# The FFN's LayerNorm tiles (`hbuf`) written by GpSimd instead of ScalarE

## The chip, the cores and the metric

The kernel runs on one core of one Trainium2 chip. The core has five engines that work side by side and meet only at semaphores: TensorE (PE; PEld is its weight load), VectorE (DVE), ScalarE (ACT), GpSimd (POOL) and SyncE (SP), the last of which only issues transfers here. Each engine takes its instructions strictly in the order in which they are written. The metric is device time in microseconds (us), median of several runs.

## What is computed

A cross-attention layer and a feed-forward layer with a learned memory, on 16 tiles of 128 tokens x 1024. Cut to what matters here:

```python
x = x + xattn(layernorm(x), ctx, ...)          # first layer
h = layernorm(x)                               # (x - mean) / sqrt(var + eps), per row
q = h @ Wq.T                                   # 64 columns
learned = gelu(h @ Wu1.T + bu1) @ Wu2.T + bu2  # 256 hidden columns
# router scores from q, top 8 of 256 slots, softmax, value rows -> aux_out
x = x + (h + gate * aux_out)                   # second layer
```

So the second LayerNorm `h` is needed twice: as the operand of a product with 320 columns (256 for `Wu1`, 64 for `Wq`), and in the sum `x + h`.

## The kernel before, in words

`X[:, b, :]` holds tile `b` (b = 0 to 15) for the whole run. The attention part runs as a software pipeline over periods `b` of four steps `i`; in period `b` the keys of tile `b`, the queries of tile `p = b - 1`, the output of tile `o = b - 2` and the normalisation of tile `e = b - 3` are worked on. There are 19 periods, so that periods 16, 17 and 18 (`B`, `B+1`, `B+2`) drain the pipeline.

The first part of the FFN, the "hidden steps", begins in period `B+1`: `early_step(b, i)` gives step 0 for `(B+1, 0)` up to step 7 for `(B+2, 3)`; steps 8 to 16 follow alone. In hidden step `s`:

- TensorE transposes `hbuf` of tile `s+1` (`h_transpose`, L543, 8 transposes into the PSUM tile `k_slot` or `q_slot`), and then multiplies tile `s` (`hidden_products`, L556, 24 matmuls of 320 columns; three per block, since operands are split in a high and a low half).
- ScalarE copies the transposed tile `s+1` out of PSUM rounded (`hT_high`, L788), runs the gelu of tile `s-1` (L792), writes `hbuf` of tile `s+2` (`h_scale`, L782: `X*rstd2 + nb2`, where `nb2 = -mean*rstd2`), and sums the weighted gelu of tile `s-1` (`unit_sum`, L796).
- VectorE makes the low half (`hT_low`, L1155), multiplies the gelu by `Wu2` (`unit_weights`, L1172, both inputs in SBUF), and adds the bias to the product of tile `s` (`unit_bias`, L1161).
- GpSimd writes `x + h` into `X` in place (`hidden_sum`, L1001: `X*(1+rstd2) + nb2`), once `h_done` says that `hbuf` has been made from the old `X`.

`hbuf` has two buffers, taken in turn, so tile `b` may be written once the transposes of tile `b-2` are done (semaphore `h_T`).

Tiles 0 and 1 are made earlier: `h_scale(0)` at the end of period `B`, after which TensorE does `h_transpose(0)` right after its last `o_pair` (L504) of that period, and `h_scale(1)` at the start of period `B+1`. GpSimd's own work at that place is `q_scale` (L967, which the transposes `q_turn` L465 wait for), a `memset` of `q_rows` (L1052), `mt_bias` (L973, which the next `o_pair` waits for), `rstd2_pow` (L987 to L994: `rstd2`, `nb2` and `1+rstd2` of one tile, five small instructions) and `norm_scale` (L978 to L982, which `o_turn` L512 waits for).

In period `B+1`, step 2, TensorE's `o_pair` has to wait until ScalarE has emptied the PSUM tile `ob` (`o_copy`, L758), and ScalarE does that after its `unit_sum`.

After the hidden steps comes a tail of top-8 selection, softmax, and output products for the 16 tiles.

Of the kernel before, what the change touches and what calls it, by code (L numbers as in the profile page):

```python
# [6 lines left out]
ALU = mybir.AluOpType  # L7
ACT = mybir.ActivationFunctionType
# [3 lines left out]
B = 16  # L12
# [24 lines left out]
def wait(engine, sem, value):  # L37

    if value > 0:
        engine.wait_ge(sem, value)  # L40
# [7 lines left out]
def attention_ffn_kernel(nc, x, ctx_rows, ctx_cols, WqT_raw, WkT_raw, Wv_rows, WoT_rows, bo_row, g_col, Wuq_cols,  # L48
# [3 lines left out]
    with ctx:  # L52
# [7 lines left out]
        X = sb("x_all", [P, B, N])  # L60
# [4 lines left out]
        rstd2 = sb("rstd2", [P, B, 1])  # L65
        nb2 = sb("nb2", [P, B, 1])
# [68 lines left out]
        hbuf = sb("hbuf", [P, 2, N], scope=ffn)  # L135
# [55 lines left out]
        def early_step(b, i):  # L191
            return 4 * (b - B - 1) + i
# [72 lines left out]
        k_moved = [sem(f"k_moved{k}") for k in range(2)]  # L265
# [31 lines left out]
        rstd2_done = sem("rstd2_done")  # L297
# [13 lines left out]
        h_done = sem("h_done")  # L311
# [46 lines left out]
        def moved(b):  # L358

            return MOVED * b - MOVED // 2 if b else 0  # L360
# [353 lines left out]
        def _(act):  # L714
# [61 lines left out]
                    last = nc.scalar.mul(mt_sb[:, b % 2, t, :], gm[:, t * C:(t + 1) * C], kscale[:, t:t + 1])  # L776
                last.then_inc(mt_copied, 1)

            def h_scale(b, k):
                act.wait_ge(nb2_done, b + 1)  # L780
                wait(act, h_T, b - 1)
                nc.scalar.activation(hbuf[:, k, :], X[:, b, :], ACT.Identity, bias=nb2[:, b, :],  # L782
                                     scale=rstd2[:, b, :]).then_inc(h_done, 1)

            def hT_high(b, k):
                act.wait_ge(h_T, b + 1)
                wait(act, units_prod, b - 1)
# [11 lines left out]
            def hidden_step(b):  # L799
                if b + 1 < B:  # L800
                    hT_high(b + 1, (b + 1) % 2)
                if has(b - 1):
                    unit_gelu(b - 1, (b - 1) % 2)
                if b + 2 < B:
                    h_scale(b + 2, b % 2)
                if b == EARLY + 3:
                    act.wait_ge(varh_step, 2)
                    nc.scalar.activation(logv[:, :], varh[:, :], ACT.Ln, bias=ones[:, 0:1]).then_inc(logv_done, 1)
                if 0 < b < B:
                    unit_sum(b - 1, (b - 1) % 2)  # L810
# [14 lines left out]
            for b in range(PERIODS):  # L825
                p, o, e = b - 1, b - 2, b - 3
                for i in range(4):
                    if i == 0 and has(o):
                        mt_scale(o)
                    if i == 0 and has(e):  # L830
                        o_copy(e, 1)
                    if i == 2 and has(o):
                        o_copy(o, 0)
                    if b == B + 1 and i == 0:
                        act.wait_ge(q_prod, 4 * B)
                        act.wait_ge(m_prod, B)
                        hT_high(0, 0)
                        h_scale(1, 1)
                    qb, qi = (p, i - 1) if i else (o, 3)
                    if has(qb):  # L840
                        q_exponential(qb, qi)
                    if 0 < b < B:
                        k_exponential(b, i)
                    if i == 1 and 0 < b and has(b + 1):
                        ctx_high(b + 1)
                    qb, qi = (p, i - 2) if i >= 2 else (o, i + 2)
                    if has(qb):
                        if qb == 0 and qi == 0:
                            act.wait_ge(k_weights, 2)
                            act.wait_ge(q_weights, 2)  # L850
                        q_copy(qb, qi)
                    if i == 0 and has(e):
                        o_square(e, 1)
                    if i == 3 and has(o):
                        o_square(o, 0)
                    if i == 1 and 0 < b < B:
                        x_layernorm(b)
                    if i == 2:
                        if has(p):
                            g_copy(p)  # L860
                        if 0 < b < B:
                            x_high(b)
                    if b == 1 and i == 0:
                        act.wait_ge(u_prod, 1)
                        nc.scalar.copy(U[:, :, :].rearrange("p h c -> p (h c)"), turn[:, :]).then_inc(u_done, 1)
                    if b == 1 and i == 1:
                        act.wait_ge(vv_prod, NSLOT // P)
                        act.wait_ge(rk_prod, 1)
                        nc.scalar.copy(VV[:, :, :].rearrange("p s (r d) -> p s r d", d=VB),
                                       ob[:, 0:2 * VB].rearrange("p (s d) -> p s d", d=VB).unsqueeze(2).broadcast_to(  # L870
                                           [P, NSLOT // P, P // VB, VB])).then_inc(vv_copied, 1)
                        nc.scalar.copy(rkT, ob[0:RDIM, NSLOT:2 * NSLOT]).then_inc(rk_copied, 1)
                        act.wait_ge(score_zeros, 1)
                        nc.scalar.mul(scoreB[0:BOT, NSLOT:2 * NSLOT], keysT,
                                      float(BOT) ** -0.5).then_inc(score_ready, 1)
                    if b == 1 and i == 3:
                        act.wait_ge(b1_prod, 1)
                        nc.scalar.mul(scoreB[0:BOT, 0:NSLOT], ob[0:BOT, 0:NSLOT],
                                      float(RDIM) ** -0.5).then_inc(score_ready, 1)
                    if b == B and i == 0:  # L880
                        act.wait_ge(k_prod, 4 * B)
                        act.wait_ge(ctx_lo_done, B)
                        nc.scalar.dma_start(Wuq_in[:, :, :], Wuq_cols).then_inc(wuq_in, 16)
                    if b == B and i == 1:
                        act.wait_ge(k_prod, 4 * B)
                        act.wait_ge(wuq_in, 16)
                        nc.scalar.copy(WuqT[0][:, :, :], Wuq_in[:, :, :]).then_inc(wuq_hi, 1)
                    if b == B and i == 3:
                        for half in range(2):
                            act.wait_ge(k_moved[half], moved(B))  # L890
                        h_scale(0, 0)
                    if early_step(b, i) >= 0:
                        hidden_step(early_step(b, i))

# [46 lines left out]
        def _(pool):  # L941
# [43 lines left out]
            def rstd2_pow(b):  # L985
# [7 lines left out]
                nc.gpsimd.tensor_scalar(nb2[:, b, :], mr2[:, :], -1.0, None, ALU.mult).then_inc(nb2_done, 1)  # L993
                nc.gpsimd.tensor_scalar(one_rstd2[:, b, :], rstd2[:, b, :], 1.0, None, ALU.add).then_inc(one_rstd2_done, 1)  # L994

            def hidden_sum(b):

                pool.wait_ge(h_done, b + 1)
                pool.wait_ge(nb2_done, b + 1)
                pool.wait_ge(one_rstd2_done, b + 1)  # L1000
                nc.gpsimd.tensor_scalar(X[:, b, :], X[:, b, :], one_rstd2[:, b, :], nb2[:, b, :], ALU.mult,  # L1001
                                        ALU.add).then_inc(y_done, 1)
# [26 lines left out]
            for b in range(PERIODS):  # L1029
                p, o, e = b - 1, b - 2, b - 3  # L1030
                for i in range(4):
                    if i == 0 and has(o):
                        mt_bias(o)
                    if i == 3 and 0 < b < B:
                        x_low(b)
                    if early_step(b, i) == 0:
                        hidden_sum(0)
                    qb, qi = (p, i - 1) if i else (o, 3)
                    if has(qb):
                        q_scale(qb, qi)  # L1040
                    if i == 0 and 0 < b < B:
                        rstd_pow(b)
                    if i == 0 and has(e - 1):
                        rstd2_pow(e - 1)
                    if i == 1 and b > 0 and has(b + 1):
                        ctx_low(b + 1)
                    if i == 1 and has(e):
                        norm_scale(e)
                    if b == B and i == 3:
                        for half in range(2):  # L1050
                            pool.wait_ge(k_moved[half], moved(B))
                        nc.gpsimd.memset(q_rows[:, :, BOT:P], 1.0).then_inc(query_ones, 1)  # L1052
                    if early_step(b, i) > 0:
                        hidden_sum(early_step(b, i))
            rstd2_pow(B - 1)
# [6 lines left out]
                                        ALU.mult).then_inc(oscale_done, 1)  # L1062

            for b in range(EARLY, B):
                hidden_sum(b)
                if b == EARLY + 2:
                    pool.wait_ge(wvu_hi, 1)
                    nc.gpsimd.tensor_tensor(WvuT_lo[:, :], WvuT_in[:, :], WvuT_hi[:, :].bitcast(F32),
                                            ALU.subtract).then_inc(wvu_lo, 1)
# [363 lines left out]
```

## Time and profile before

| what | value |
|---|---|
| median of 3 runs | 640.03 us (640.01 to 640.49) |
| the profiled execution's own time | 640.05 us |
| its span in the trace | 638.1 us |
| PE busy | 615.7 us (96%) |
| DVE busy | 540.2 us (85%) |
| ACT busy | 416.9 us (65%) |
| POOL busy | 371.7 us (58%) |
| chain that ended last | PE 92% of the span |

The 1.95 us between the span and the execution's own time lie around the profile. The chain of waits is followed back from the last instruction; where it is nearly all one engine, that engine's order and pauses set the time, and the other engines' loads matter only where that engine waits for them. The hidden steps with the start of their preparation lie between 500 and 589 us of the span.

### The profile page before, as it was taken

How to read it: one execution, taken by the hardware profiler on the slowest of the kernel's cores; microseconds unless marked ns; L12 is line 12 of the kernel's file. 1: busy time of each engine (PE TensorE's matmuls, PEld its weight loads, DVE VectorE, ACT ScalarE, POOL GpSimd, SP SyncE). 2: the span in 40 equal slices, each digit the busy share in tenths (PEclk: the TensorE clock that was granted, in tenths of full speed). 3: DMA queues.
4: the chain of work that ended last, by engine and by line, in shares of the span. 5: the costliest groups of instructions: out<-in, count | busy, mean ns of one | idle time of the engine just before them, and what ended most of it. 6: DMA issues, size and time to landing. Idle time of an engine off the chain costs nothing.

```text
span 638.1 us, 11806 instructions
## 1 busy us (share of the span) xinstructions
PE 615.7 (96%) x3974; PEld 541.3 (85%) x3974; DVE 540.2 (85%) x757; ACT 416.9 (65%) x844; POOL 371.7 (58%) x369
## 2 busy tenths in 40 slices
PE   4899999999999999999999999999999999999796
PEld 3778888888888988888888988888888999999574
DVE  5989898989989898989898989898986745756997
ACT  5566676666666766666676767676664866773793
POOL 4954464848474748474747575756646456421394
PEclk9999999999999999999999999999999999999999
DMA  8943543444444444444444344543245100000056
GB/s 283 252 121 101 144 110 118 118 125 115 126 109 126 111 134 114 126 115 122 112 129 135 108 109 127 150 109 99 72 104 149 42 1 2 1 2 1 34 230 264
DMA packets 52010, 72.57 MB, mean 114 GB/s; under 512 B 10112, under 2 KB 42400, under 8 KB 51696
## 3 DMA queue, kind: packets, MB, share of 16 engines
q1 hardware_dynamic: 50912, 68.07, 37.3%
q0 software_dynamic: 896, 2.45, 1.3%
q10 hardware_dynamic: 144, 1.31, 0.6%
q8 instruction: 32, 0.52, 0.4%
q14 instruction: 26, 0.21, 0.1%
HBM read 29.85 MB, written 8.39 MB: 60 GB/s over the span
## 4 chain that ended last, share of the span: by engine, by line
PE 92%; DVE 3%; SPq 2%; issue 1%; ACT 1%; DMA 1%; DVEq 0%; ACTq 0%
PE ob L504 18%; PE gm L481 17%; PE turn L465 8%; PE k_slot L439 5%; PE q_slot L439 5%; PE k_slot L441 5%; PE q_slot L441 4%; PE gm L556 4%; PE k_slot L440 4%; PE q_slot L440 4%; PE turn L556 4%; PE gm L490 2%; PE turn L512 2%; SPq L383 2%; PE turn L680 1%
## 5 line engine op out<-in xcount | busy, mean ns | idle before, releaser
L967 POOL TENSOR_TENSOR qs_sb<-qs_sb,qrec 128x1024 f32<-128x1024 f32 x64 | 122.0, 1906 | 150.0 <-DVE qrec L1137 150.0
L736 ACT ACTIVATE ek<-k_slot,nkm 128x1024 f32<-128x1024 f32 x62 | 69.1, 1114 | 95.7 <-DVE nkm L1102 95.4
L504 PE MATMUL ob<-mt_sb,q_hd 128*128 128x128 f32 x1024 | 126.4, 277 | 0.6 <-ACT o_sb L758 0.5
L504 PEld LDWEIGHTS ob<-mt_sb,q_hd 128*128 128x128 f32 x1024 | 121.8, 192 | 5.2 <-issue 3.6
L481 PE MATMUL gm<-ekT,ctxT 128*128 128x256 f32 x512 | 118.2, 379 | 1.1 <-DMA ekT<-kt 1.1
L481 PEld LDWEIGHTS gm<-ekT,ctxT 128*128 128x128 f32 x512 | 97.0, 190 | 16.2 <-DMA ekT<-kt 1.5
L746 ACT ACTIVATE qs_sb<-qs_sb 128x1024 f32<-128x1024 f32 x64 | 68.5, 1071 | 31.6 <-DVE qs_sb L1126 31.6
L1102 DVE TENSOR_REDUCE nkm<-k_slot 128x1 f32<-128x1024 f32 x62 | 74.2, 1198 | 16.3 <-PE k_slot L441 16.3
L1133 DVE TENSOR_REDUCE qsum<-qs_sb 128x16 f32<-128x1024 f32 x64 | 76.9, 1202 | 4.1 <-ACT qs_sb L746 4.1
L1126 DVE TENSOR_TENSOR qs_sb<-q_slot,qm 128x1024 f32<-128x1024 f32 x64 | 78.4, 1225 | 2.2
L1109 DVE STREAM_TRANSPOSE kt<-ek 128x1024 f32<-128x1024 f32 x64 | 78.5, 1227 | 0.0
L1123 DVE TENSOR_REDUCE qm<-q_slot 128x16 f32<-128x1024 f32 x64 | 75.6, 1181 | 0.0
L465 PEld LDWEIGHTS turn<-ident,qs_sb 128*128 128x128 f32 x512 | 59.6, 140 | 8.1 <-issue 0.5
L465 PE MATMUL turn<-ident,qs_sb 128*128 128x128 f32 x512 | 66.4, 272 | 0.0
L751 ACT COPY q_hd<-turn 128x1024 f32<-128x1024 f32 x64 | 64.3, 1005 | 2.9 <-PE turn L465 2.9
L439 PE MATMUL k_slot<-ctx_hi,WkT_hi 128*128 128x512 f32 x124 | 54.7, 441 | 9.7 <-DVE ctx_lo L1287 7.5
L439 PE MATMUL q_slot<-WqT_hi,xn_hi 128*128 128x512 f32 x128 | 55.6, 434 | 0.0
L441 PE MATMUL q_slot<-WqT_lo,xn_hi 128*128 128x512 f32 x128 | 50.5, 395 | 0.0
L440 PE MATMUL q_slot<-WqT_hi,xn_lo 128*128 128x512 f32 x128 | 49.9, 390 | 0.0
L441 PE MATMUL k_slot<-ctx_lo,WkT_hi 128*128 128x512 f32 x124 | 49.3, 398 | 0.0
L440 PE MATMUL k_slot<-ctx_hi,WkT_lo 128*128 128x512 f32 x124 | 49.0, 396 | 0.0
L961 POOL TENSOR_TENSOR xn_lo<-xn,xn_hi 128x1024 fp32r<-128x1024 f32 x16 | 38.3, 2396 | 14.9 <-ACT xn_hi L730 14.9
(200 smaller groups left out, 1227.4 us busy)
## 6 DMA issues: line engine op xcount, KB each, us to landing
ekT<-kt SPq DMA_DIRECT2D x496, 64.0 KB, 2.0
ctx_in<-ctx_rows SPq DMA_DIRECT2D x16, 512.0 KB, 4.6
x_all<-x SPq DMA_DIRECT2D x16, 512.0 KB, 3.6
ctxT<-ctx_cols SPq DMA_DIRECT2D x16, 512.0 KB, 4.1
out<-q_hd SPq DMA_DIRECT2D x15, 512.0 KB, 2.6
Wuq_in<-Wuq_cols ACTq DMA_DIRECT2D x1, 1280.0 KB, 6.5
x_all<-values_cols POOLq DMA_DIRECT2D x1, 1024.0 KB, 8.6
ekT<-kt POOLq DMA_DIRECT2D x16, 64.0 KB, 4.4
```

Source lines behind the costliest of these rows:

```text
L439: nc.tensor.matmul(dst, lhs[0], rhs[0], start=True, stop=False)
L440: nc.tensor.matmul(dst, lhs[1], rhs[0], start=False, stop=False)
L441: return nc.tensor.matmul(dst, lhs[0], rhs[1], start=False, stop=True)
L465: last = nc.tensor.transpose(turn[:, (2 * t + n) * P:(2 * t + n + 1) * P], qs_sb[:, i % 2, n * HALF + t * P:n * HALF + (t + 1) * P], ident ...
L481: last = nc.tensor.matmul(gm[:, cols], ctxT[:, b % 2, j, :], ekT[:, 2 * half:2 * half + 2, :, j * BLK:(j + 1) * BLK], start=(j == 0), stop ...
L504: last = nc.tensor.matmul(ob[:, (j % 4) * C:(j % 4 + 1) * C], q_hd[:, t, j * P:(j + 1) * P], mt_sb[:, b % 2, t, :], start=(t == 0), stop=( ...
L967: nc.gpsimd.tensor_tensor(e, e, qrec[:, i % 2, :].unsqueeze(2).broadcast_to([P, PAIR, DH]), ALU.mult).then_inc(q_mul, 1)
L1102: V.tensor_reduce(nkm[:, i:i + 1], k_psum(b, i)[:, :], AX, ALU.max, negate=True).then_inc(k_max, 1)
L1109: V.transpose(kt[:, i, :], ek[:, i % 2, :]).then_inc(k_T, 1)
L1123: V.tensor_reduce(qm[:, :], q, AX, ALU.max).then_inc(q_max, 1)
L1126: V.tensor_tensor(qs_sb[:, i % 2, :].rearrange("p (m d) -> p m d", d=DH), q, qm[:, :].unsqueeze(2).broadcast_to([P, PAIR, DH]), ALU.subtra ...
L1133: V.tensor_reduce(qsum[:, :], qs_sb[:, i % 2, :].rearrange("p (m d) -> p m d", d=DH), AX, ALU.add).then_inc(q_sum, 1)
```

## The change

`h_scale` is taken out of ScalarE's program, in all of its 16 places. `h_make` is put into GpSimd's: one `tensor_scalar` with two per-row scalars, `rstd2` and `nb2`, multiply then add, into the same `hbuf` buffer, and it gives the same semaphore `h_done`. `hidden_sum` stays as it was. Everything on TensorE, VectorE and SyncE stays in its order.

```diff
-            def h_scale(b, k):
-                act.wait_ge(nb2_done, b + 1)
-                wait(act, h_T, b - 1)
-                nc.scalar.activation(hbuf[:, k, :], X[:, b, :], ACT.Identity, bias=nb2[:, b, :],
-                                     scale=rstd2[:, b, :]).then_inc(h_done, 1)
...
@@ ScalarE, hidden_step
-                if b + 2 < B:
-                    h_scale(b + 2, b % 2)
@@ ScalarE, period B + 1, step 0
                         hT_high(0, 0)
-                        h_scale(1, 1)
@@ ScalarE, end of period B
-                    if b == B and i == 3:
-                        for half in range(2):
-                            act.wait_ge(k_moved[half], moved(B))
-                        h_scale(0, 0)
@@ GpSimd
+            def h_make(b):
+                pool.wait_ge(nb2_done, b + 1)
+                pool.wait_ge(rstd2_done, b + 1)
+                wait(pool, h_T, b - 1)
+                nc.gpsimd.tensor_scalar(hbuf[:, b % 2, :], X[:, b, :], rstd2[:, b, :], nb2[:, b, :], ALU.mult,
+                                        ALU.add).then_inc(h_done, 1)
...
                     if early_step(b, i) == 0:
+                        h_make(1)
                         hidden_sum(0)
...
                     if b == B and i == 3:
                         for half in range(2):
                             pool.wait_ge(k_moved[half], moved(B))
+                        h_make(0)
                         nc.gpsimd.memset(q_rows[:, :, BOT:P], 1.0).then_inc(query_ones, 1)
+                    if early_step(b, i) >= 0:
+                        h_make(early_step(b, i) + 2)
                     if early_step(b, i) > 0:
                         hidden_sum(early_step(b, i))
...
             for b in range(EARLY, B):
+                if b + 2 < B:
+                    h_make(b + 2)
                 hidden_sum(b)
```

On GpSimd, where period `B` ends and `B+1` begins, the order before is this (a row's L is its line, `qs_sb` is the query tile of `q_scale`, `mt_sb` that of `mt_bias`):

```order
L967 TENSOR_TENSOR qs_sb<-qs_sb,qrec 128x1024 [waits q_rec] x2
L1052 MEMSET q_rows 128x16x64 [waits k_moved1,k_moved0]
L973 TENSOR_TENSOR mt_sb<-mt_sb,bo_bc 128x128 [waits bo_halved,mt_copied]
L1001 TENSOR_SCALAR x_all<-x_all,one_rstd2,nb2 128x1024 [waits one_rstd2_done,nb2_done,h_done]
L967 TENSOR_TENSOR qs_sb<-qs_sb,qrec 128x1024 [waits q_rec]
```

And now, with the lines of the changed kernel:

```order
L954 TENSOR_TENSOR qs_sb<-qs_sb,qrec 128x1024 [waits q_rec] x2
L987 TENSOR_SCALAR hbuf<-x_all,rstd2,nb2 128x1024 [waits nb2_done,rstd2_done,k_moved1,k_moved0]
L1048 MEMSET q_rows 128x16x64
L960 TENSOR_TENSOR mt_sb<-mt_sb,bo_bc 128x128 [waits bo_halved,mt_copied]
L987 TENSOR_SCALAR hbuf<-x_all,rstd2,nb2 128x1024 [waits rstd2_done,nb2_done]
L995 TENSOR_SCALAR x_all<-x_all,one_rstd2,nb2 128x1024 [waits one_rstd2_done,nb2_done,h_done]
L954 TENSOR_TENSOR qs_sb<-qs_sb,qrec 128x1024 [waits q_rec]
```

Tile 0 is now made behind the second `q_scale` and ahead of the memset and of `mt_bias`; tile 1 behind `mt_bias`.

On GpSimd a little later, from the last instruction of `rstd2_pow` in period `B+1`, through `norm_scale`, to the sum of tile 1; before:

```order
L994 TENSOR_SCALAR one_rstd2<-rstd2 128x1
L978 TENSOR_SCALAR l2c<-l2 128x8 [waits l2_sum]
L980 TENSOR_TENSOR rn<-l2c,half_neg 128x8 [waits l2_clamped]
L982 TENSOR_TENSOR o_sb<-o_sb,rn 128x1024 [waits rn_pow]
L1001 TENSOR_SCALAR x_all<-x_all,one_rstd2,nb2 128x1024 [waits one_rstd2_done,nb2_done,h_done] x3
```

And now:

```order
L981 TENSOR_SCALAR one_rstd2<-rstd2 128x1
L987 TENSOR_SCALAR hbuf<-x_all,rstd2,nb2 128x1024 [waits h_T,rstd2_done,nb2_done]
L965 TENSOR_SCALAR l2c<-l2 128x8 [waits l2_sum]
L967 TENSOR_TENSOR rn<-l2c,half_neg 128x8 [waits l2_clamped]
L969 TENSOR_TENSOR o_sb<-o_sb,rn 128x1024 [waits rn_pow]
L987 TENSOR_SCALAR hbuf<-x_all,rstd2,nb2 128x1024 [waits h_T,rstd2_done,nb2_done]
L995 TENSOR_SCALAR x_all<-x_all,one_rstd2,nb2 128x1024 [waits one_rstd2_done,nb2_done,h_done]
```

Tile 2 is made ahead of `norm_scale`, tile 3 behind it, and from here on a tile is made ahead of each sum.

On ScalarE, hidden step 1, between the copy of transposed tile 2 and `o_copy`; before:

```order
L788 CAST hT_hi<-k_slot 128x1024 [waits units_prod,h_T]
L792 ACT_TABLE_LOAD
L792 ACTIVATE units<-units 128x256 [waits units_biased]
L782 ACTIVATE hbuf<-x_all,nb2,rstd2 128x1024 [waits h_T,nb2_done]
L796 ACTIVATE units,learned<-units 128x256 [waits gelu_weighted]
L758 COPY o_sb<-ob 128x512 [waits l2_sum,o_T,o_prod]
```

And now:

```order
L782 CAST hT_hi<-k_slot 128x1024 [waits units_prod,h_T]
L786 ACT_TABLE_LOAD
L786 ACTIVATE units<-units 128x256 [waits units_biased]
L790 ACTIVATE units,learned<-units 128x256 [waits gelu_weighted]
L758 COPY o_sb<-ob 128x512 [waits l2_sum,o_T,o_prod]
```

`unit_sum` and `o_copy` now follow the gelu directly.

## Rows read from the trace of the kernel before

**Rows 1.** Windows; columns: PE, PEld, DVE, ACT, POOL busy (count), PEclk, DMA share, GB/s.
```profile
500.00:518.00 18.00, 17.93 (x150) 17.54 (x147) 10.74 (x16) 14.98 (x28) 13.63 (x15) 1.00 0.13 37
518.00:520.00 2.00, 1.46 (x13) 1.25 (x12) 1.63 (x3) 1.02 (x4) 1.71 (x2) 1.00 0.00 0
520.00:573.00 53.00, 53.00 (x394) 52.70 (x393) 30.78 (x62) 37.31 (x73) 21.77 (x24) 1.00 0.01 2
573.00:575.00 2.00, 1.08 (x10) 0.87 (x9) 1.24 (x6) 0.94 (x3) 1.20 (x1) 1.00 0.00 0
```

**Rows 2.** Timeline of PE's weight loads; columns: start us, us, instruction, idle before.
```profile
502.21 0.91 PEld L543 LDWEIGHTS k_slot<-ident,hbuf 128*128 128x128 f32 x8
...
504.26 1.86 PEld L504 LDWEIGHTS ob<-mt_sb,q_hd 128*128 128x128 f32 x16 [0.27 <-issue]
...
519.14 1.86 PEld L504 LDWEIGHTS ob<-mt_sb,q_hd 128*128 128x128 f32 x16 [0.75 <-issue]
...
574.25 0.30 PEld L575 LDWEIGHTS gm<-logsum,ones 128*128 128x128 f32 x2 [1.13 <-issue]
```

**Rows 3.** Chain that ended last, 517 to 520; columns: start us, us, what.
```profile
518.06 0.49 ACT units L796 x2
518.56 0.48 ACT o_sb L758
```

**Rows 4.** Timeline of POOL, 500 to 520.
```profile
500.98 1.90 POOL L967 TENSOR_TENSOR qs_sb<-qs_sb,qrec 128x1024 f32<-128x1024 f32 x1 [8.42 <-DVE qrec L1137]
502.82 0.95 POOL L1052 MEMSET q_rows<- 128x1024 f32 x1
503.74 0.46 POOL L973 TENSOR_TENSOR mt_sb<-mt_sb,bo_bc 128x128 f32<-128x128 f32 x1
...
508.19 1.90 POOL L967 TENSOR_TENSOR qs_sb<-qs_sb,qrec 128x1024 f32<-128x1024 f32 x1 [2.82 <-DVE qrec L1137]
...
515.90 3.81 POOL L1001 TENSOR_SCALAR x_all<-x_all,one_rstd,nb 128x1024 f32<-128x1024 f32 x3
```

**Rows 5.** Timeline of ACT: three instructions of the hidden steps.
```profile
503.47 1.01 ACT L788 CAST hT_hi<-k_slot 128x1024 fp32r<-128x1024 f32 x1 [0.36 <-PE k_slot L543]
...
516.93 1.24 ACT L782 ACTIVATE hbuf<-x_all,nb,rstd 128x1024 f32<-128x1024 f32 x1
...
569.66 1.01 ACT L788 CAST hT_hi<-q_slot 128x1024 fp32r<-128x1024 f32 x1
```

**Rows 6.** One line's instructions (ns min/median/max, first and last start), then groups (count, busy us, mean ns).
```profile
L1001 POOL TENSOR_SCALAR x_all<-x_all,one_rstd,nb x16: 1192/1198/1456, 504.2 to 578.2; 128x1024 f32<-128x1024 f32 x16
```
```profile
L782 ACT ACTIVATE hbuf<-x_all,nb,rstd 128x1024 f32<-128x1024 f32 x16 | 19.8, 1234 | 0.0
```
```profile
L961 POOL TENSOR_TENSOR xn_lo<-xn,xn_hi 128x1024 fp32r<-128x1024 f32 x16 | 38.3, 2396 | 14.9 <-ACT xn_hi L730 14.9
```

**Rows 7.** Timelines of POOL and of DVE: where `unit_weights` (L1172) meets GpSimd's work.
```profile
556.20 2.42 POOL L1068 TENSOR_TENSOR WvuT_lo<-WvuT_in,WvuT_hi 128x1024 fp32r<-128x1024 f32 x1 [1.00 <-DVE WvuT_hi L1343]
558.61 1.37 POOL L1001 TENSOR_SCALAR x_all<-x_all,one_rstd,nb 128x1024 f32<-128x1024 f32 x1
```
```profile
517.05 0.48 DVE L1172 TENSOR_TENSOR units<-units,Wu 128x256 f32<-128x256 f32 x1 [0.51 <-ACT units L792]
...
558.02 0.88 DVE L1172 TENSOR_TENSOR units<-units,Wu 128x256 f32<-128x256 f32 x1
...
572.44 0.43 DVE L1172 TENSOR_TENSOR units<-units,Wu 128x256 f32<-128x256 f32 x1 [0.51 <-ACT units L792]
573.18 0.42 DVE L1161 TENSOR_TENSOR units<-turn,bu 128x256 f32<-128x256 f32 x1 [0.32 <-PE turn L556]
```

**Rows 8.** When tiles 2 and 10 are transposed, and POOL's work before tile 10.
```profile
513.20 1.04 PE L543 MATMUL k_slot<-ident,hbuf 128*128 128x128 f32 x8
```
```profile
554.92 0.87 PE k_slot L543 x8
```
```profile
550.09 2.38 POOL L1001 TENSOR_SCALAR x_all<-x_all,one_rstd,nb 128x1024 f32<-128x1024 f32 x2
```

## The prediction

> **What bounds the kernel now.** I read the page first: PE is busy 96% of the span and the chain that ended last is 92% PE. The change touches only the stretch from about 500 us on, so I then took that stretch alone. In the windows [rows 1] PE is busy 17.93 of 18.00 us, then 1.46 of 2.00, then 53.00 of 53.00, then 1.08 of 2.00; the granted clock is 1.00 in all four, which is the upper of its two levels. So from 500 to 575 PE has two real pauses and is otherwise full. Whatever delays PE here is therefore not made up later, except in one of those pauses. ACT (37.31 of 53.00) and POOL (21.77 of 53.00) both have room: moving load from one to the other is worth nothing by itself. The question is only where PE waits for one of them.
>
> PE's weight loads show the pauses [rows 2]: 0.27 us before the load at 504.26 (the first `o_pair` of period B+1; it waits for `mt_bias`, which ends at 503.74+0.46 = 504.20 [rows 4]), 0.75 us before 519.14, and 1.13 us before 574.25. The chain [rows 3] says what the second waits for: ScalarE's `unit_sum` and then its `o_copy` of `ob`. The third waits for VectorE, from its `unit_bias` at 573.18 [rows 7] through two copies.
>
> **What is removed.** 16 `h_scale`, 1234 ns each, 19.8 us of ScalarE [rows 6]. Of this only one lies on PE's path: the one at 516.93 [rows 5], between the gelu and `unit_sum` of hidden step 1. It isn't worth its 1.24 us there, since `unit_sum` also needs `unit_weights` on VectorE, which ends at 517.05+0.48 = 517.53 [rows 7]. `unit_sum` starts at 518.06 [rows 3] and could start at about 517.56. Gain: **0.50 us** of the 0.75 us pause. The other 15 are hidden under PE, and in the third pause no `h_scale` is between PE and the VectorE work.
>
> **What is added on GpSimd.** 16 `h_make`. The nearest rows are the 16 `hidden_sum`: same engine, same operation form with two per-row scalars, same shape, 1192 to 1456 ns, median 1198 [rows 6]. The far bound from above is a GpSimd operation with two tensor inputs, 2396 ns [rows 6]. I take 1.19 us, since the form is identical but for the output buffer and the median lies at the lower end. That is 16 x 1.19 = 19 us more on an engine that is 59% idle between 520 and 573 [rows 1].
>
> **First tile: the term that sets the sign.** Before, ScalarE made tile 0 early enough for PE, which loads it at 502.21 [rows 2] with no pause. Now it stands on GpSimd behind the `q_scale` of 500.98+1.90 = 502.88 [rows 4], which itself came after 8.42 us of waiting for VectorE, so it can't be earlier. The next instruction began at 502.82, so tile 0 runs from about 502.86 to 504.05. PE's load followed `mt_bias` by 0.06 us (504.20 to 504.26), so PE loads tile 0 at 504.11 instead of 502.21: **+1.90 us**. PE is in order; nothing behind it can pass.
>
> Behind it on GpSimd: memset 0.95 and `mt_bias` 0.46 [rows 4], so `mt_bias` ends at 504.05+0.95+0.46 = 505.46. PE gets to its `o_pair` two groups of 8 transposes after tile 0. Before, this was at 504.26-0.27 = 503.99; now 503.99+1.90 = 505.89. The old wait of 0.27 us is gone: **-0.27 us**, delay now 1.63. Tile 1 is ready at 505.46+1.19 = 506.65, before PE wants it (over 507.6).
>
> **Tiles 2 and 3 and the ScalarE pause.** The copy of transposed tile 0 moves from 503.47 [rows 5] to 505.37, but ScalarE saves the `h_scale` behind it, so the exponential that leads to the `q_scale` at 508.19 moves by 1.90-1.14 = 0.76; the low-half work on VectorE in between makes it some 0.88. `q_scale` is then at 509.07 and everything behind it on GpSimd is 0.88 later, plus 1.19 for tile 2. Tile 2 is ready at about 514.0; PE wants it at 513.20+1.63 = 514.83 [rows 8], a margin of 0.8 us. `norm_scale` then ends at 515.90+0.88+1.19 = 517.97 [rows 4], still before PE's `o_turn`, some 1.2 us later. Tile 3 runs on GpSimd from 517.97 to 519.16.
>
> That collides with `unit_weights`. Of its 16 instances most take 0.42 us, but the one at 558.02 took 0.88 us [rows 7]: GpSimd's `WvuT_lo` ran until 558.62, and `unit_weights` ended 0.28 us after that. The GpSimd sum that began at 558.61 took 1.37 instead of 1.20 us. So a VectorE operation with two SBUF inputs and a GpSimd one exclude each other, whoever comes second waits. The Trainium skill ("SBUF — State Buffer", section "Who interferes with whom") states it as a rule that speaks against this change: a DVE instruction with two SBUF inputs contends with a GpSimd instruction that reads SBUF, and the second to issue blocks until the first is done. The trace agrees (0.88 against 0.42 us); if the two shared the port instead, the sum would be rival (a)'s.
>
> In hidden step 1 `unit_weights` would start at 517.05+1.63 = 518.68, inside tile 3's 517.97 to 519.16, and end at 519.16+0.28 = 519.44 instead of 519.16: **+0.28 us** on `unit_sum`, `o_copy` and PE. Delay after this pause: 1.63-0.50+0.28 = **1.41 us**.
>
> **Tiles 4 to 15.** From here GpSimd makes a tile as soon as `h_T` frees its buffer, so a tile is ready most of a step (about 4.5 us) before PE wants it. The tightest later place is tile 10, behind `rstd2_pow` of the last tile: before, that was over at 550.09 [rows 8], now at 551.5, and tile 10 is ready at 552.7; PE wants it at 554.92+1.41 = 556.3 [rows 8]. Cost: none. If the cover were gone, PE would pay the shortfall once.
>
> **The VectorE pause.** In PE's third pause `unit_bias` at 573.18 starts 0.32 us after VectorE is free from the `unit_weights` of 572.44 [rows 7]. The copy of transposed tile 13, at 569.66 [rows 5], gives the time at which GpSimd may make tile 15: 569.66+1.41 = 571.07. Then tile 15 and the sums of tiles 13 and 14 run back to back: until 572.26, 573.45, 574.64. `unit_weights` would start at 573.85, in the sum of tile 14, and end at 574.64+0.28 = 574.92, while `unit_bias` would otherwise start at 574.59: **+0.3 us** on VectorE's copies and on PE. In all other steps such a wait (at most one GpSimd instruction, 1.2 us) either meets slack before `unit_bias` or, from tile 8 on, the second of two PSUM buffers.
>
> Sum: +1.90 - 0.27 - 0.50 + 0.28 + 0.30 = **+1.71 us**. After 589 us the order of all engines is as before and everything hangs on the last hidden products, so it all moves by the sum. Against the profiled execution's 640.05 us (0.02 above the median): 641.76, forecast 641.8 us.
>
> **Rivals.**
> (a) *Tile 0 is late, but the collisions on VectorE cost nothing*, because they fall between two GpSimd instructions. For it: the meeting times rest on sums of six to ten durations, a few tenths decide. Against it: tile 3's window holds `unit_weights` with 0.7 us to one side and 0.5 to the other. Then +1.90-0.27-0.50 = +1.13 us: 641.2 us, within 0.2% of before. This is the case on the other side of "slower": it decides at PE's first load of tile 0, and a gain would need that load before 503.5 or so.
> (b) *GpSimd becomes PE's supplier with too little margin*: tile 2 has 0.8 us. If `h_make` takes 1.46 us, the longest sum in the trace, PE's first wait grows by 0.26, tile 2's margin falls to about 0.3, and further `unit_weights` are blocked; in steps 3 to 7 the products wait for one PSUM tile, so a late `unit_bias` reaches PE with some tenths each. +2.1 to +3 us: 642.1 to 643.0. At 2.4 us each, the far bound, PE would lose 1.2 more at tile 0 and about 1.2 at tile 2: 644.3; with an identical form in the rows I give this next to nothing.
> (c) *ScalarE's relief is worth more than it seems*: all of the 0.75 us pause vanishes (+1.90-0.27-0.75 = +0.88) and nothing collides: 640.9 or a little less. For a real gain (below 638.8) some other PE pause would have to be ScalarE's, and rows 1 leave no room for one. The change may also do nothing at all only if tile 0 were not waited for, which the `q_scale` ahead of it excludes.
>
> **How the numbers follow.** Forecast case (1.3 to 2.1 us) 0.48; (a) 0.30; (b) 0.15; (c) 0.07. About 0.2%, 1.28 us, is what a measurement of this kernel can tell from no change; it lies at 641.3 us, close under the forecast. Slower: 0.48 + 0.15, less a little for the low edge, 0.61. Same: 0.30 and most of (c), 0.36. Faster: 0.03. Range: from (a)'s and (c)'s 640.9 to the upper part of (b), 642.9.
>
> **What the changed profile would show.** PE's load of tile 0 at 504.1 with a pause of about 1.9 us before it, released by GpSimd's `h_make`; `h_make` at 1.19 to 1.2 us; no pause before the next `o_pair`; 0.4 to 0.6 us instead of 0.75 before the `o_pair` of 519; one long `unit_weights` (0.7 to 0.8 us) in that place and one over 1 us near 574. The last hidden products end 1.7 us later than 589.4. I'd be wrong if tile 0's load isn't the largest new pause, if a later tile's load shows a pause on GpSimd, or if something in the tail takes up the delay.

## The result, and the profile after

| | before | changed |
|---|---|---|
| median, us | 640.5 (20 runs, 639.61 to 644.36) | 642.61 (20 runs, 641.12 to 645.65) |
| ratio, 95% interval | | 1.003 (1.0018 to 1.0041) |
| profiled execution's time, us | 640.05 | 641.59 |
| its span, us | 638.1 | 639.7 |
| ACT busy, us | 416.9 | 399.2 |
| POOL busy, us | 371.7 | 391.7 |

The changed kernel is slower by 0.3%, as forecast, and the interval lies wholly above 1. The forecast of 641.8 us was reckoned from a before of 640.03 to 640.05 us; over 20 runs the medians are 640.5 and 642.61, 2.1 us apart, so that the new one lies 0.8 us above the forecast and inside the range. The profiled execution is 1.54 us longer; of the change it shows a little more than that, since it reached the stretch in question 0.27 us earlier (below).

PE's weight loads of the changed kernel, from 500 to 530; columns as in [rows 2]:

```profile
500.16 1.86 PEld L504 LDWEIGHTS ob<-mt_sb,q_hd 128*128 128x128 f32 x16 [0.17 <-issue]
503.92 0.85 PEld L543 LDWEIGHTS k_slot<-ident,hbuf 128*128 128x128 f32 x8 [1.89 <-issue]
504.74 0.90 PEld L465 LDWEIGHTS turn<-ident,qs_sb 128*128 128x128 f32 x8
505.61 1.86 PEld L504 LDWEIGHTS ob<-mt_sb,q_hd 128*128 128x128 f32 x16
...
514.44 0.91 PEld L543 LDWEIGHTS k_slot<-ident,hbuf 128*128 128x128 f32 x8
...
520.42 1.86 PEld L504 LDWEIGHTS ob<-mt_sb,q_hd 128*128 128x128 f32 x16 [0.67 <-issue]
```

There is a new pause of 1.89 us before tile 0's load, where [rows 2] has none; the pause of 0.27 before the next `o_pair` is gone; the one at ScalarE's `o_copy` is 0.67 instead of 0.75 us. GpSimd in the same place, against [rows 4]:

```profile
500.71 1.90 POOL L954 TENSOR_TENSOR qs_sb<-qs_sb,qrec 128x1024 f32<-128x1024 f32 x1 [8.59 <-DVE qrec L1137]
502.60 1.20 POOL L987 TENSOR_SCALAR hbuf<-x_all,rstd,nb 128x1024 f32<-128x1024 f32 x1
503.74 0.95 POOL L1048 MEMSET q_rows<- 128x1024 f32 x1
504.66 0.45 POOL L960 TENSOR_TENSOR mt_sb<-mt_sb,bo_bc 128x128 f32<-128x128 f32 x1
```

Tile 0 (`hbuf`, L987) runs behind `q_scale`, which waited 8.59 us for VectorE, and PE's load at 503.92 follows its end at 503.80. VectorE's `unit_weights` at the two places named in the prediction, and what follows the second, against [rows 7]:

```profile
518.41 0.88 DVE L1172 TENSOR_TENSOR units<-units,Wu 128x256 f32<-128x256 f32 x1 [0.51 <-ACT units L786]
...
573.70 1.23 DVE L1172 TENSOR_TENSOR units<-units,Wu 128x256 f32<-128x256 f32 x1 [0.51 <-ACT units L786]
574.86 0.41 DVE L1161 TENSOR_TENSOR units<-turn,bu 128x256 f32<-128x256 f32 x1
```

0.88 for 0.48 us, and 1.23 for 0.43 us; the second leaves no idle time before `unit_bias`, where there were 0.32 us. The cause stands in GpSimd's timeline:

```profile
517.80 1.22 POOL L987 TENSOR_SCALAR hbuf<-x_all,rstd,nb 128x1024 f32<-128x1024 f32 x1
519.00 1.36 POOL L995 TENSOR_SCALAR x_all<-x_all,one_rstd,nb 128x1024 f32<-128x1024 f32 x1
...
571.09 1.20 POOL L987 TENSOR_SCALAR hbuf<-x_all,rstd,nb 128x1024 f32<-128x1024 f32 x1 [2.22 <-PE q_slot L543]
572.27 3.74 POOL L995 TENSOR_SCALAR x_all<-x_all,one_rstd,nb 128x1024 f32<-128x1024 f32 x3
```

**A measure for all that follows.** Executions differ, by up to 2.8 us among those traced here, in when they reach the work near 500 us, before anything that the change touches. The four that come to it after 502 us have in common that TensorE's granted clock, the column PEclk, fell to its lower level near 20 us. In the second trace of the changed kernel (columns as in [rows 1]):

```profile
20.00:30.00 10.00, 10.00 (x53) 8.39 (x54) 8.13 (x9) 3.17 (x4) 9.32 (x20) 0.83 0.94 236
```

In the other nine traces this row has 1.00. So I take the stretch **S**, from PE's load of the last `o_pair` of period B (500.43 before, 500.16 changed) to the start of VectorE's last `unit_bias` (589.40 and 591.06):

```profile
589.40 0.42 DVE L1161 TENSOR_TENSOR units<-turn,bu 128x256 f32<-128x256 f32 x1 [1.48 <-PE turn L556]
```
```profile
591.06 0.42 DVE L1161 TENSOR_TENSOR units<-turn,bu 128x256 f32<-128x256 f32 x1 [1.48 <-PE turn L556]
```

The first row is of before, the second of the changed kernel. S is 88.97 us before and 90.90 after: **+1.93 us**. The second trace of the changed kernel has 90.88, though it reached S 1.9 us later.

### The profile page after: what moved, and what is told of

Same layout as the page of the kernel before. It is cut to its first block, busy times and chain, and to the rows that moved or that the text cites. A ratio compares the mean times of both kernels' runs of the same rounds, so it can differ in the third digit from the quotient of the medians.

```text
span 639.7 us, 11807 instructions
## 1 busy us (share of the span) xinstructions
PE 615.0 (96%) x3974; PEld 540.9 (85%) x3974; DVE 542.5 (85%) x757; ACT 399.2 (62%) x828; POOL 391.7 (61%) x385
## 4 chain that ended last, share of the span: by engine, by line
PE 91%; issue 3%; ACT 2%; DVE 2%; DMA 1%; POOL 1%; SPq 0%; DVEq 0%; POOLq 0%; ACTq 0%
PE ob L504 18%; PE gm L481 17%; PE turn L465 9%; PE k_slot L439 5%; PE q_slot L439 5%; PE q_slot L441 5%; PE k_slot L441 4%; PE q_slot L440 4%; PE k_slot L440 4%; PE gm L556 4%; PE turn L556 4%; PE gm L490 2%; PE turn L512 2%; PE k_slot L543 1%; PE turn L680 1%
```

## The experiments

The theory (A) is the prediction's: one late tile on PE's path, a gain at ScalarE's pause, two collisions on VectorE, all else hidden. The rival (B) is that GpSimd's load and the collisions along the whole stretch cost the time. All S below are from one profiled execution each. Each edit is shown against the changed kernel unless it says otherwise.

### Tile 0 in GpSimd's idle time

```diff
+                    if b == B and i == 3:
+                        for half in range(2):
+                            pool.wait_ge(k_moved[half], moved(B))
+                        h_make(0)
                     if early_step(b, i) == 0:
                         h_make(1)
...
                     if has(qb):
                         q_scale(qb, qi)
...
-                        for half in range(2):
-                            pool.wait_ge(k_moved[half], moved(B))
-                        h_make(0)
                         nc.gpsimd.memset(q_rows[:, :, BOT:P], 1.0).then_inc(query_ones, 1)
```

> The changed kernel, with one thing moved: GpSimd makes tile 0 ahead of the second q_scale of the end of period B, in the 8.6 us in which it waited for VectorE there, not behind it; all 16 tiles stay on GpSimd. Measure: the stretch S from PE's weight load of the last o_pair of period B to the start of VectorE's last unit_bias, 88.97 us in the kernel before (500.43 to 589.40) and 90.90 us in the changed one (500.16 to 591.06). Theory A (one late tile on PE's path, all else hidden but two collisions): PE has no pause at tile 0; mt_bias is waited for again (0.27); S = 88.97 - 0.5 (ScalarE's pause) + 0.4 (collision at tile 15) = 88.9, time ratio to before 1.000 +- 0.001. Theory B (19 us more on GpSimd and collisions all along the hidden steps cost the time): S stays at 90 or more, ratio 1.002 or more.

Measured: S = 88.97 us, ratio 0.9995 (0.9984 to 1.0006, 10 runs). GpSimd of this kernel:

```profile
492.47 1.19 POOL L987 TENSOR_SCALAR hbuf<-x_all,rstd,nb 128x1024 f32<-128x1024 f32 x1
500.90 1.90 POOL L954 TENSOR_TENSOR qs_sb<-qs_sb,qrec 128x1024 f32<-128x1024 f32 x1 [7.23 <-DVE qrec L1138]
```

Tile 0 is ready 8 us early, the wait for VectorE is shorter by about what the tile takes (7.23 us, against 8.42 before and 8.59 in the changed kernel), and the whole loss is gone although all 16 tiles are still on GpSimd. Theory B falls. S agrees with 88.9 within 0.1: PE's pause at `o_copy` is 0.37 instead of 0.75 us, and the second collision takes as much back (PE's third pause is 1.51 instead of 1.13 us). So with tile 0 out of the way the change gains and loses nothing.

### Tile 0 alone on GpSimd

Against the kernel before; `h_make` is the changed kernel's.

```diff
@@ ScalarE
                         hT_high(0, 0)
+                        act.wait_ge(h_done, 1)
                         h_scale(1, 1)
...
-                    if b == B and i == 3:
-                        for half in range(2):
-                            act.wait_ge(k_moved[half], moved(B))
-                        h_scale(0, 0)
@@ GpSimd, end of period B
                             pool.wait_ge(k_moved[half], moved(B))
+                        h_make(0)
                         nc.gpsimd.memset(q_rows[:, :, BOT:P], 1.0).then_inc(query_ones, 1)
```

> The kernel before, with tile 0 alone moved to GpSimd, at the place where the change puts it; the other 15 stay on ScalarE. S is 88.97 us before, 90.90 us with the whole change. Theory A: PE pauses 1.9 to 2.0 us at tile 0, gets back 0.27 at mt_bias, and ScalarE's pause of 0.75 stays: S = 88.97 + 1.98 - 0.27 = 90.7, ratio about 1.0026: one tile in 16 costs nearly all that the change costs. Theory B (load and collisions): S = 89.2 or less.

Measured: S = 90.60 us (+1.63), where theory A had 90.7 and B at most 89.2. PE's pause at tile 0 is 1.89 us, and the pause of 0.75 at `o_copy` is back. So one tile of 16 makes +1.63 of the +1.93. The ratio, 1.0039 (1.0024 to 1.0054) over 4 runs, is above the expected 1.0026, though its interval takes that in. The profiled execution shows where the rest lies: its span is 3.8 us longer than that of before, of which 1.63 is S. 1.62 it had lost when it reached S (502.05 for 500.43, one of the four with the low clock near 20 us), and some 0.5 it lost behind S, where the clock was low from 596 to 602 us.

### Tile 0 made twice

```diff
                         for half in range(2):
                             pool.wait_ge(k_moved[half], moved(B))
+                        pool.wait_ge(rstd2_done, 1)
+                        pool.wait_ge(nb2_done, 1)
+                        nc.gpsimd.tensor_scalar(hbuf[:, 0, :], X[:, 0, :], rstd2[:, 0, :], nb2[:, 0, :], ALU.mult,
+                                                ALU.add).then_inc(h_twice, 1)
+                        pool.wait_ge(h_twice, 1)
                         h_make(0)
```

> The changed kernel, with the instruction that makes tile 0 done twice, one after the other (1.2 us more, nothing else changed). Theory A: PE has nothing that could hide it, so S grows by the full 1.2 to 1.3 us, from 90.90 to 92.1, and tile 2's margin stays, since everything on GpSimd and PE moves together; ratio to before 1.0048. Theory B: the pause at tile 0 is made up in the later pauses: S grows by 0.5 or less.

Measured: PE's pause 3.19 us, S = 93.39 us, ratio 1.0077 (1.0049 to 1.0106, 4 runs). Neither theory has that: A said 92.1, or 92.2 with the measured pause (90.90 + 3.19 - 1.89), and is short by 1.2 us. The windows of this kernel show where they are:

```profile
506.00:508.00 2.00, 0.81 (x8) 0.84 (x9) 0.31 (x2) 0.00 (x0) 2.00 (x3) 1.00 0.73 254
508.00:510.00 2.00, 2.00 (x13) 2.00 (x12) 0.59 (x1) 1.64 (x2) 2.00 (x3) 0.54 0.03 8
510.00:512.00 2.00, 2.00 (x13) 2.00 (x13) 1.97 (x3) 2.00 (x8) 0.71 (x1) 0.61 0.00 0
512.00:514.00 2.00, 2.00 (x19) 2.00 (x18) 0.04 (x1) 0.94 (x5) 1.87 (x1) 1.00 0.00 0
```

Behind the pause, once PE works again, the granted clock is 0.54 and 0.61 for some 3.5 us: the lower of its two levels, 1.2 GHz, for most of that time. PE's weight loads show what that costs:

```profile
507.15 0.86 PEld L544 LDWEIGHTS k_slot<-ident,hbuf 128*128 128x128 f32 x8 [3.19 <-issue]
507.98 1.53 PEld L466 LDWEIGHTS turn<-ident,qs_sb 128*128 128x128 f32 x8
509.50 2.86 PEld L505 LDWEIGHTS ob<-mt_sb,q_hd 128*128 128x128 f32 x16
512.28 0.91 PEld L544 LDWEIGHTS q_slot<-ident,hbuf 128*128 128x128 f32 x8
...
524.85 1.86 PEld L505 LDWEIGHTS ob<-mt_sb,q_hd 128*128 128x128 f32 x16 [0.23 <-issue]
```

From tile 0's load to tile 1's they take 512.28 - 507.15 = 5.13 us, where the changed kernel takes 507.40 - 503.92 = 3.48: **1.65 us** for the low clock. S shows only 1.2 of them, because the first collision is gone in this trace: `unit_weights` takes 0.43 instead of 0.88 us there, and the pause at `o_copy` is 0.23 instead of 0.67. The low clock is a cost of a long pause that theory A lacks; I call it theory C. One of the four executions had a mean clock of 0.999, and its time was 643.06 us, against 643.1 from 641.82, the median of the changed kernel's executions with such a clock (below), plus 1.3.

### No collisions

```diff
                     if early_step(b, i) >= 0:
+                        if early_step(b, i) == 1:
+                            pool.wait_ge(gelu_weighted, 1)
                         h_make(early_step(b, i) + 2)
...
                     h_make(b + 2)
+                if b == B - 2:
+                    pool.wait_ge(gelu_weighted, B - 3)
                 hidden_sum(b)
```

> The changed kernel, with two waits added on GpSimd: tile 3 is made only after VectorE's first unit_weights, and the sum of tile 14 only after its thirteenth. Nothing is left out. Theory A (a VectorE operation with two SBUF inputs waits for a running GpSimd one): unit_weights falls from 0.88 to about 0.45 us in the first place and from 1.23 to 0.42 in the second; PE gets 0.4 us back at each; S = 90.90 - 0.8 = 90.1, with PE's pause at tile 0 unchanged at 1.9. Rival: the long unit_weights are hidden behind something else that ends as late, and S stays at 90.9.

Measured: S = 90.04 us, 0.86 less than the changed kernel. The two `unit_weights`:

```profile
519.06 0.43 DVE L1176 TENSOR_TENSOR units<-units,Wu 128x256 f32<-128x256 f32 x1 [0.51 <-ACT units L786]
525.77 1.23 DVE L1176 TENSOR_TENSOR units<-units,Wu 128x256 f32<-128x256 f32 x1
...
573.91 0.43 DVE L1176 TENSOR_TENSOR units<-units,Wu 128x256 f32<-128x256 f32 x1 [0.51 <-ACT units L786]
```

The collisions moved (the one at 525.77 is now 1.23 us, and costs nothing), and where they are gone PE has its time back. So it is the place that decides, not the number of collisions: PE's two later pauses are 0.23 and 1.12 us, where the changed kernel has 0.67 and 1.53. PE's pause at tile 0 stays 1.89 us.

### ScalarE's relief by itself

Against the kernel before: tile 3 is made after `o_copy`.

```diff
-                if b + 2 < B:
+                if b + 2 < B and b != 1:
                     h_scale(b + 2, b % 2)
...
                         o_copy(o, 0)
+                        if b == B + 1:
+                            h_scale(3, 1)
```

> The kernel before, with one instruction moved on ScalarE: tile 3 is made after the o_copy of period B+1, step 2, not between gelu and unit_sum. It measures the gain of ScalarE's relief by itself. Theory A: PE's weight load of that o_pair pauses 0.25 us instead of 0.75, S = 88.97 - 0.5 = 88.5. Rival (relief is worth its full duration, or nothing): S = 88.2 (the whole pause), or 88.97.

Measured: PE's pause before that `o_pair` is 0.22 instead of 0.75 us, S = 88.46 us (-0.51). One of 16 removed `h_scale` is worth 0.51 us of its 1.24, since VectorE's `unit_weights` comes next.

### Tiles 4 to 15 made twice

```diff
                 wait(pool, h_T, b - 1)
+                if b >= 4:
+                    nc.gpsimd.tensor_scalar(hbuf[:, b % 2, :], X[:, b, :], rstd2[:, b, :], nb2[:, b, :], ALU.mult,
+                                            ALU.add).then_inc(h_twice, 1)
+                    pool.wait_ge(h_twice, b - 3)
                 nc.gpsimd.tensor_scalar(hbuf[:, b % 2, :], X[:, b, :], rstd2[:, b, :], nb2[:, b, :], ALU.mult,
```

> The changed kernel, with the instruction that makes a tile done twice for tiles 4 to 15 (12 x 1.2 = 14.4 us more work for GpSimd in the hidden steps, nothing left out). Theory A: tiles 4 to 15 have margins of 1.2 us and more, so PE never pauses for them; only the times at which GpSimd meets VectorE's unit_weights shift: S = 90.90 with -0.4 to +0.8. Theory B (GpSimd's load counts): S grows by several us, with pauses at the loads of hbuf.

Measured: S = 90.46 us, 0.44 less than the changed kernel, with 14 us more work on GpSimd, and no pause of PE at any `hbuf` load but tile 0's (1.89). Two `unit_weights` of this kernel:

```profile
564.30 2.44 DVE L1177 TENSOR_TENSOR units<-units,Wu 128x256 f32<-128x256 f32 x1
...
574.11 0.47 DVE L1177 TENSOR_TENSOR units<-units,Wu 128x256 f32<-128x256 f32 x1 [0.51 <-ACT units L787]
```

The longest collision of all, 2.44 us (with `WvuT_lo`, which takes 2.39 us), costs nothing, while the one at the 13th `unit_weights` has gone by chance, and that is the 0.4 us. Theory B is out.

### Two repaired versions

The first joins the repairs: tile 0 and the memset ahead of `q_scale`, and the two waits of the kernel without collisions.

```diff
+                    if b == B and i == 3:
+                        for half in range(2):
+                            pool.wait_ge(k_moved[half], moved(B))
+                        h_make(0)
+                        nc.gpsimd.memset(q_rows[:, :, BOT:P], 1.0).then_inc(query_ones, 1)
                     if early_step(b, i) == 0:
                         h_make(1)
```

> The changed kernel with three things put right: tile 0 and the memset of q_rows are ahead of the second q_scale on GpSimd, tile 3 is made after VectorE's first unit_weights, and the sum of tile 14 after its thirteenth. Theory A: no pause at tile 0, none at mt_bias (-0.27), ScalarE's pause 0.25 (-0.5), no collision: S = 88.97 - 0.77 = 88.2, ratio to before 0.9988. Theory B (GpSimd's load): S above 89.

Measured: S = 88.11 us, ratio 0.9986 (0.9975 to 0.9996, 10 runs).

The second leaves out the wait for tile 3 and takes `unit_sum` out of `o_copy`'s way on ScalarE:

```diff
-                if 0 < b < B:
+                if 1 < b < B:
                     unit_sum(b - 1, (b - 1) % 2)
...
                         o_copy(o, 0)
+                        if b == B + 1:
+                            unit_sum(0, 0)
```

> As the last, but the collision at tile 3 is left in and made harmless: ScalarE does the first unit_sum after the o_copy of period B+1, step 2, so that o_copy waits neither for VectorE nor for that sum. Theory A: that pause of PE (0.75 us before) vanishes whole: S = 88.97 - 0.27 - 0.75 = 87.95, ratio to before 0.998 to 0.999. If S is above 88.2, something else ends as late there.

Measured: S = 87.87 us (-1.10), ratio **0.9976** (0.9964 to 0.9987, 12 runs): faster than both kernels. PE's loads of this version have no pause left where before there were two:

```profile
502.14 0.91 PEld L543 LDWEIGHTS k_slot<-ident,hbuf 128*128 128x128 f32 x8
503.02 0.91 PEld L465 LDWEIGHTS turn<-ident,qs_sb 128*128 128x128 f32 x8
503.89 1.86 PEld L504 LDWEIGHTS ob<-mt_sb,q_hd 128*128 128x128 f32 x16
...
517.09 0.94 PEld L512 LDWEIGHTS turn<-ident,o_sb 128*128 128x128 f32 x8
518.00 1.86 PEld L504 LDWEIGHTS ob<-mt_sb,q_hd 128*128 128x128 f32 x16
```

So with all tiles on GpSimd the kernel can be some 1 us faster than before. That this is owed to their being there isn't shown. The gain is made of an earlier `mt_bias` (0.27) and the whole pause at `o_copy` (0.75), and both come from the order of the work: 0.51 of the second was had above with every tile on ScalarE, and an earlier memset and a later `unit_sum` weren't tried on the kernel before. The change with tile 0 alone put right gained nothing (S = 88.97).

### Theory C: the length of the pause

Tile 0's work is made longer by half a tile and by two tiles (the diff is as for "made twice", once with `0:512` as the columns, once with the instruction there two times), and the changed kernel runs again beside them.

> The changed kernel, with half of tile 0 (512 of its 1024 columns) written once more ahead of it; nothing left out. PE's pause at tile 0 goes from 1.9 to about 2.6 us. Theory A (only the wait counts): S = 90.90 + 0.7 = 91.6 in every execution, ratio to before 1.0041. Theory C (after a long pause TensorE's clock is granted at its lower level for some microseconds, as it was at 508 to 512 us behind the pause of 3.2 us): in part of the executions 1 to 2 us more, with a mean clock of 0.995 or less; the more often, the longer the pause.

> The changed kernel, with the instruction that makes tile 0 done three times; PE's pause there goes to 4.4 us. Theory A: S = 90.90 + 2.5 = 93.4, ratio 1.0069. Theory C: the low clock behind the pause in most executions, S = 94.7 or more, ratio 1.008 to 1.010.

> The changed kernel as it is, on the same chip as the two with the longer pauses. Theory A: its executions with a mean clock of 0.999 lie 1.6 to 1.9 us above those of the kernel before with the same clock, and no more of them have a lower clock than of the kernel before. Theory C: more of its executions have a lower mean clock (about 0.995 and less) than of the kernel before, which adds some tenths to its median over the 1.93 us that the trace shows.

| PE's pause at tile 0 | kernels traced | lower clock at it | from tile 0's load to tile 1's, us | S against 90.90 + (pause - 1.89) | ratio to before |
|---|---|---|---|---|---|
| none | tile 0 in idle time, both repaired | no | | | 0.9995, 0.9986, 0.9976 |
| 1.89 us | changed (twice), tile 0 alone, no collisions, tiles twice | no, in five traces | 3.48 | 90.88 and 90.90 for the changed | 1.003 and 1.0036 for the changed |
| 2.77 us | half a tile more | yes, 508 to 512 | 5.13 | 93.00 for 91.8: 1.2 | 1.0059 (1.0039 to 1.008) |
| 3.19 us | tile 0 twice | yes, 508 to 512 | 5.13 | 93.39 for 92.2: 1.2 | 1.0077 (1.0049 to 1.0106) |
| 4.48 us | tile 0 thrice | yes, 505 to 512 | 6.06 | 95.65 for 93.5: 2.2 | 1.01 (1.0078 to 1.0122) |

Windows of the kernel with half a tile more, then of that with tile 0 thrice:

```profile
508.00:510.00 2.00, 2.00 (x14) 2.00 (x12) 0.10 (x1) 1.14 (x2) 2.00 (x4) 0.61 0.29 117
510.00:512.00 2.00, 2.00 (x12) 2.00 (x11) 2.00 (x2) 2.00 (x5) 1.13 (x1) 0.53 0.03 8
```
```profile
504.00:506.00 2.00, 0.00 (x0) 0.00 (x0) 0.41 (x2) 0.00 (x0) 1.90 (x2) 0.77 0.77 254
506.00:508.00 2.00, 1.43 (x7) 1.46 (x8) 0.00 (x0) 0.00 (x0) 2.00 (x4) 0.50 0.01 2
```

The low clock comes with the pauses of 2.77 us and more in all three traces, and with the pauses of 1.89 us in none of five. It costs PE 1.65, 1.65 and 2.58 us; S is longer by only 1.2, 1.2 and 2.2, since in all three the first collision is gone (`unit_weights` 0.47, 0.43 and 0.42 us). The times agree: 3 of 8 executions with half a tile more kept a mean clock of 0.999 or more and took 642.93 to 643.31 us, the other five 644.19 to 647.1. The last is the profiled one, and it was low near 20 us and in the tail as well: a mean clock doesn't say where.

Is the clock part of what the change costs? The same low level stands in seven of the 13 traces in the tail, after PE has been nearly idle, with and without a pause at tile 0. In the last repaired version:

```profile
590.00:592.00 2.00, 0.13 (x2) 0.00 (x0) 1.97 (x9) 1.71 (x6) 0.00 (x0) 1.00 0.00 0
592.00:594.00 2.00, 1.31 (x6) 1.10 (x7) 1.43 (x7) 0.87 (x3) 0.00 (x0) 0.64 0.00 0
594.00:596.00 2.00, 2.00 (x6) 1.16 (x6) 1.77 (x9) 1.43 (x5) 0.00 (x0) 0.51 0.00 0
```

PE's longest pause just ahead of that place is 2.30 or 2.31 us in all 13 traces, also in the six that stay at 1.00, those of before and changed among them. So the length of one pause doesn't decide alone, and the table's rows aren't a limit for other places.

Of the kernel before, 25 of the 53 executions beside these experiments had a mean clock of 0.998 or more, with a median of 640.11 us; of the changed kernel it was 7 of 30 (the 20 of the result and 10 beside the last experiments), with a median of 641.82. In such executions the change therefore costs **1.71 us**; within the last experiments alone, 3 against 8 of them, it is 1.8. Over all executions the medians are 640.58 and 642.74, 2.16 us apart. The 0.4 us between would fit a somewhat more frequent low clock in the changed kernel. These counts don't show it: within the last experiments they are 3 of 10 against 8 of 17, and neither of its two traces has the low clock at tile 0 (the second has it near 20 us, where the kernels are the same). It stays open.

## Why the prediction was right

The forecast was 641.8 us, +1.71 over the profiled 640.05; the changed kernel's executions with a mean clock of 0.998 or more lie 1.71 us above those of before, its trace shows +1.93 in S, and its median of 642.61 is inside the range. The mechanism is the predicted one, term by term; that the figure comes back to the hundredth is luck, since the seven executions behind it go from 641.12 to 642.84 us, and in S the two collisions together are 0.22 us larger than forecast.

- **Tile 0, +1.90.** Measured 503.92 - (502.21 - 0.27) = +1.98. `h_make` took 1.20 us, and PE's load followed its end by 0.12 us, not by the 0.06 taken from `mt_bias`. With tile 0 moved into GpSimd's idle time the term is gone; alone on GpSimd it makes S +1.63 together with the next.
- **`mt_bias`, -0.27.** No pause is left, and the `o_pair` is 505.61 - (504.26 - 0.27) = 1.62 late, forecast 1.63. Two small misses cancel here: tile 0 was 0.08 later than forecast, and the 16 transposes behind the pause had their loads done in 1.69 instead of 1.78 us.
- **ScalarE, -0.50, and the first collision, +0.28.** The relief alone measured -0.51. The collision was mis-sized: 0.88 against 0.48 us, +0.40. GpSimd reached tile 3 0.1 us later than reckoned (517.80 + 0.27 = 518.07 for 517.97), which makes the wait longer by as much. That comes from the step whose 1.14 and 0.88 us the prediction takes from no row that it shows: the `q_scale` began at 508.89 + 0.27 = 509.16, 0.97 later than before. Together the delay went from 1.62 to 520.42 - (519.14 - 0.27) = 1.55 us, forecast 1.41.
- **The second collision, +0.30.** `unit_bias` is 574.86 - (573.18 - 0.27) = 1.95 late, so +0.40. Without both collisions S falls by 0.86.
- **Tiles 1 to 15 hidden.** Right: PE has no pause at any of their loads, and twelve of them can be made twice.
- **The tail moves as it is.** S and the span agree: 1.93 - 0.27 = 1.66 against 639.7 - 638.1 = 1.6.

Rival (a), no cost of collisions, was wrong: they fell as the sum had them. Rival (b) was right in one thing, collisions in more steps (eight of the 16 `unit_weights` took over 0.5 us), and wrong in that they would reach PE. In (c) the relief is as small as said. What no case had was the clock: it would have mattered with a tile of 2.4 us, the far bound, where the prediction's 644.3 us lacks what the pause of 3.19 us brought on top (1.65 us on PE, 1.2 in S).

## What to carry to other kernels

When work is moved to an emptier engine, look not at its load but at what stands directly ahead of it in that engine's order, and how long that waits: here one tile of 16, put behind an instruction that had waited 8.6 us, made +1.63 of the +1.93 us, and put ahead of it, it cost nothing. Then go through the few places where the bounding engine pauses anyway, since only there does relief or a collision count. And before crediting a repaired version to the move, try the same repairs without the move. Take the effect from a stretch with fixed ends on the engines' own instructions: it showed steps of 0.3 us that the spread of whole executions hides.

## What was unexpected of the hardware

- With a pause of TensorE of 2.77, 3.19 and 4.48 us its granted clock was at the lower level for some 3 to 7 us, which cost PE 1.65, 1.65 and 2.58 us beyond the pause; with 1.89 us it wasn't, in five traces. Not every execution did it with 2.77 and 3.19 us: four of 12 kept a mean clock of 0.999 or more. In work with more gaps shorter pauses went with it: the clock was low behind one of 2.31 us in the tail in seven of 13 traces, and near 20 us, behind a matmul pause of 1.80 us, in four of 13.
- Where GpSimd's instructions follow each other without a gap, VectorE's waiting operation still gets in between two of them: no `unit_weights` of the changed kernel took longer than 1.23 us, about one of GpSimd's 1.2 us instructions. The sum that ran behind the second collision took 1.37 instead of 1.21 us. The one of 2.44 us, in the kernel with tiles 4 to 15 made twice, met `WvuT_lo` with its 2.39 us.
